# An attention pipeline whose routing follows one body sooner, with GpSimd's list of work and the ends of four stages rearranged

## The chip, the cores and the metric

The kernel runs on one NeuronCore of a Trainium2 chip. Its engines work at the same time, each on its own list of instructions: TensorE (PE; PEld is its loading of weights), VectorE (DVE), ScalarE (ACT), GpSimd (POOL) and SyncE (SP). They wait for each other through semaphores. The metric is the time of one execution on the device, in microseconds (us); the median of several executions counts.

## The reference

Four layers follow each other, each of them added to a running `x` of 32 batches x 256 rows x 128 columns: attention with an MLP, a mixture of experts, a recurrence, and the mixture of experts again with the same weights.

```python
x = x + attention(layernorm(x))     # 16 heads of 8, causal mask with a bias by distance; then relu MLP 128-512-128
x = x + experts(layernorm(x))       # 8 experts 128-256-128 (silu(gate) * up), the top 2 of the softmax, shares renormalised
x = x + recurrence(layernorm(x))    # gated scan over the rows, with its own layernorm
x = x + experts(layernorm(x))
```

For a mixture of experts `layernorm(x)` of each row is multiplied with the router's weights (128 x 8), the two largest of the 8 logits choose the experts, and the row's result is the sum of those two experts' outputs, weighted by their shares.

## The kernel before, in words

The program runs in stages that follow each other: a setup, attention, the experts ("first_"), the recurrence, the experts ("second_"), and a closing sum (`combine`). Each stage is a block in which every engine has a list of work written out by hand. A stage ends when all engines have reached its end: each engine drains its queue, all meet, and the semaphores are cleared. `phase` (L52 to L73) does the last part: it lets all engines meet in a barrier (L71), clears the semaphores (L72) and lets them meet again (L73).

**Attention** is a pipeline over 32 batches. Each engine's list is a function `body(b, n)`, called for `b` from -3 up to 32 plus `FULL` less one. In one body TensorE works at several batches at once: the scores of batch `b`, the maxima of `b + 1` and `b + 2`, the projection of `b + 3`, the MLP of `b - 2`, and the routing of batches further behind. A helper does nothing where its batch doesn't exist. Results of TensorE go to PSUM banks; two of them, T and W, are shared by many small matrix products. The tables `T_USES` and `W_USES` (L640 and L641) tell each user's place in the bank's turns and how many batches it lags, since the semaphores count by that.

Routing in attention works as follows, with the lag in bodies behind `b`:

- `finish(b - 2)` (L1094, VectorE) writes the finished `x` of a batch into `xres`.
- `row_stats` and `row_moments(b - 3)` (L1111, L1118, L1120, VectorE) give mean and variance; `row_root` and `row_apply(b - 3)` (L1511, L1523, GpSimd) turn them into normalised rows `d_rows`.
- `row_T` and `router(b - 4)` (L908, L917, TensorE) transpose the rows and multiply them with the router's weights; `take_rowT` and `take_logits(b - 4)` (L1329, L1338, ScalarE) take the results from PSUM.
- `sort`, `number`, `pick`, `members(b - 5)` (L175 to L193, VectorE) find the two largest logits; `rank(b - 5)` (L211, L214, TensorE) counts the rows that go to each expert; `place_a` to `place_d(b - 5)` (L220 to L248, VectorE) turn that into each row's place in a table in device memory. From `sort` on, the work is done once for two batches.
- `scatter` (L1543, GpSimd) sends the rows to those places by indirect DMAs, 128 rows each, the first choice (`b - 6`) and the second one (`b - 7`) in four DMAs each for every two batches. Before the second choice `relabel` (L244) overwrites the number that each row carries with it.

GpSimd has more in its body: `roots` and `norm_apply(b + 3)` (L1434, L1445) for the layernorm before attention, which wait for VectorE's `arg` of L997, and `second_root` and `second_apply(b - 1)` (L1472, L1482) for the layernorm before the MLP, followed by four short groups of additions.

**The experts** (`run_dispatched`) go over 72 tiles of 256 places: they load the rows of a tile with their expert's weights, multiply, and scatter the results back by indirect DMAs (L1669). ScalarE's function there is Silu (L1747); in the recurrence it uses a sigmoid (L2184) and an exponential. A function that isn't in the table loaded last needs an ACT_TABLE_LOAD first. The recurrence routes as well, and scatters at L2077. At the end of attention, of both runs of experts and of the recurrence, GpSimd waits until all its scatters have landed.

## Time and profile before

| | us |
|---|---|
| median of 3 runs | 1771.74 |
| lowest and highest | 1770.59, 1792.68 |
| profiled execution | 1777.81 |
| its span, first to last instruction | 1776.1 |
| mean granted clock of TensorE in it | 0.859 of full speed |

| stage | from, to (us of the span) |
|---|---|
| setup | 0, 87 |
| attention: first bodies without scatters | 87, 258 |
| attention: full bodies with scatters | 258, 833 |
| attention: the last batches leave the pipeline | 833, 908 |
| experts, first | 908, 1181 |
| recurrence | 1181, 1460 |
| experts, second | 1460, 1730 |
| closing sum | 1730, 1776 |

The profile was taken from one execution, so its parts add up to that execution's time and not to the median. A row of the timeline has the start, the duration, the engine, the line of the program, the operation, what it writes and reads, and in brackets how long the engine was idle before it and what released it. "x4" after a row means that four such instructions follow each other. An engine's name with a "q" is its queue: branches, drains and the issuing of DMAs. Neighbouring instructions of VectorE overlap by about 0.1 us.

### The profile page before, as it was taken

The numbers are of one execution on the slowest core, as the hardware profiler recorded it, in microseconds if no ns is written. First come the engines' busy times: TensorE is split into PE (matmuls) and PEld (weight loads), VectorE is DVE, ScalarE is ACT, GpSimd is POOL, SyncE is SP. The second block draws the span as 40 slices with busy tenths as digits, with TensorE's granted clock in tenths as the row PEclk, the third lists the DMA queues.
The fourth block names the chain that finished last, engine by engine and source line by source line (L and its number), as shares of the span: only waits on it lengthen the run. The fifth ranks groups of instructions, "written<-read, shape, count | busy, mean of one in ns | idle before, by whom it ended". The sixth has DMA issues, their size and how long they took to land. (4 is left out here: it accounts for less than half of the span.)

```text
span 1776.1 us, 37650 instructions
## 1 busy us (share of the span) xinstructions
PE 1367.7 (77%) x11633; PEld 1112.0 (63%) x11633; DVE 1253.9 (71%) x3903; ACT 782.6 (44%) x1751; POOL 960.0 (54%) x1156
## 2 busy tenths in 40 slices
PE   3699999999999999997447878847767618787850
PEld 2467777777677777765347878835555408787850
DVE  4379998989888888885455555548888835565637
ACT  1135555545445544544134444426666615444420
POOL 2214556656666566654645555533777754555540
PEclk9569999989899999998568998968787758988985
DMA  7101111111111111111232222211222122222218
GB/s 212 44 34 41 46 46 49 46 49 52 43 49 49 43 52 52 52 34 43 89 86 76 76 72 74 76 51 53 73 74 73 51 67 77 78 74 75 80 51 284
DMA packets 101873, 121.99 MB, mean 69 GB/s; under 512 B 18168, under 2 KB 81712, under 8 KB 101424
## 3 DMA queue, kind: packets, MB, share of 16 engines
q1 hardware_dynamic: 72592, 77.73, 14.7%
q0 software_dynamic: 17408, 36.21, 6.0%
q10 hardware_dynamic: 11680, 5.66, 1.2%
q8 instruction: 98, 1.61, 0.4%
q14 instruction: 95, 0.78, 0.1%
HBM read 49.72 MB, written 44.72 MB: 53 GB/s over the span
## 5 line engine op out<-in xcount | busy, mean ns | idle before, releaser
L1020 DVE TENSOR_REDUCE mx<-max_banks 128x6 f32<-128x768 f32 x256 | 243.1, 950 | 59.9 <-PE max_banks L769 46.0
L1049 DVE TENSOR_TENSOR ebuf<-score_banks,region 128x768 f32<-128x768 f32 x256 | 243.3, 950 | 27.3 <-PE score_banks L795 24.0
L1277 ACT ACTIVATE region<-ebuf 128x768 f32<-128x768 f32 x256 | 216.3, 846 | 101.4 <-DVE ebuf L1049 98.9
L1669 POOL DMA_INDIRECT choice_rows<-first_yo,first_xg x144 | 139.2, 967 | 132.5 <-DVE first_yo L1789 98.0
L1669 POOL DMA_INDIRECT choice_rows<-second_yo,second_xg x144 | 138.8, 964 | 130.5 <-DVE second_yo L1789 93.8
L2077 POOL DMA_INDIRECT expert_rows<-d_rows,z_d_index x128 | 130.7, 1021 | 38.8 <-issue 31.7
L1543 POOL DMA_INDIRECT expert_rows<-d_rows,a_d_index x128 | 129.1, 1009 | 36.9 <-issue 32.1
L757 PE MATMUL max_banks<-identb,region 128*128 128x128 bf16 x512 | 106.6, 231 | 29.5 <-DVE mx L1020 21.8
L1434 POOL TENSOR_TENSOR rs<-arg,neghalf 128x4 f32<-128x4 f32 x32 | 33.1, 1035 | 174.1 <-DVE arg L997 174.1
L814 PE MATMUL bankO<-region,vaug 128*32 128x256 f32 (+1 forms) x2048 | 124.5, 350 | 2.8 <-ACT region L1277 1.8
L1747 ACT ACTIVATE first_silu<-first_bgu,first_biases 128x256 f32<-128x256 f32 x144 | 63.6, 477 | 130.8 <-issue 48.4
L1781 DVE SCALAR_TENSOR_TENSOR first_hT<-first_bgu,first_biases,first_silu 128x256 f32<-128x256 f32 x144 | 65.0, 478 | 79.4 <-ACT first_silu L1747 58.0
L1747 ACT ACTIVATE second_silu<-second_bgu,second_biases 128x256 f32<-128x256 f32 x144 | 64.1, 477 | 128.7 <-issue 60.3
L1709 PE MATMUL second_by<-region,second_hT 128*128 x576 | 86.9, 300 | 41.8 <-DVE second_hT L1781 41.3
L1709 PE MATMUL first_by<-region,first_hT 128*128 x576 | 87.8, 301 | 37.6 <-DVE first_hT L1781 36.1
L1781 DVE SCALAR_TENSOR_TENSOR second_hT<-second_bgu,second_biases,second_silu 128x256 f32<-128x256 f32 x144 | 65.1, 478 | 72.0 <-ACT second_silu L1747 38.8
L791 PE MATMUL score_banks<-region_r 32*128 32x256 f32 x512 | 99.5, 386 | 18.2 <-DVE ebuf L1049 18.0
L1709 PEld LDWEIGHTS second_by<-region,second_hT 128*128 128x128 f32 x576 | 78.4, 211 | 47.5 <-issue 47.5
L1709 PEld LDWEIGHTS first_by<-region,first_hT 128*128 128x128 f32 x576 | 78.8, 212 | 45.2 <-issue 45.1
L761 PE MATMUL max_banks<-identb,region 128*128 128x128 bf16 x512 | 105.5, 229 | 0.0
L759 PE MATMUL max_banks<-identb,region 128*128 128x128 bf16 x512 | 105.5, 229 | 0.0
L765 PE MATMUL max_banks<-region_r 32*128 32x256 f32 x512 | 103.5, 401 | 0.0
(326 smaller groups left out, 4318.6 us busy)
## 6 DMA issues: line engine op xcount, KB each, us to landing
region_r<-region_r SPq DMA_DIRECT2D x192, 128.0 KB
first_xg<-expert_rows SPq DMA_DIRECT2D x72, 132.0 KB
second_xg<-expert_rows SPq DMA_DIRECT2D x72, 132.0 KB
z_rows<-choice_rows SPq DMA_DIRECT2D x32, 256.0 KB
c_rows<-choice_rows SPq DMA_DIRECT2D x16, 512.0 KB
out<-xres ACTq DMA_DIRECT2D x16, 256.0 KB
choice_rows<-first_yo,first_xg POOLq DMA_INDIRECT x144
choice_rows<-second_yo,second_xg POOLq DMA_INDIRECT x144
```

What stands on the lines that cost most here:

```text
L757: nc.tensor.matmul(r[:, hh, 0:P], biasb[:, h, P:2 * P], identb[:], start=True, stop=False, skip_group_check=True)
L759: nc.tensor.matmul(r[:, hh, P:2 * P], biasb[:, h, 0:P], identb[:], start=False, stop=False, skip_group_check=True)
L814: last = nc.tensor.matmul(bankO[VW * i:VW * (i + 1), g // 2, out:lo + 2 * P], vaug[:, n, kt, h, :], p32[:, (h // 2) % 4, h % 2, cols], sta ...
L1020: nc.vector.reduce_max(mx[:, n, places:places + 5:4, :], max_banks[:, :, 0:BK].rearrange("p h (k c) -> p h k c", k=3), AXX).then_inc(maxed ...
L1049: nc.vector.tensor_tensor(ebuf[:, half_of_ebuf(c, j), :, :], score_banks[:, :, 0:BK], bias32[:, plain(j), :], ALU.add).then_inc(scores_fre ...
L1277: nc.scalar.activation(p32[:, j % 4, :, :], ebuf[:, half_of_ebuf(c, j), :, :], ACT.Exp).then_inc(exped, 1)
L1543: pool.indirect_dma_start(slots_dram, bass.IndirectOffsetOnAxis(ap=d.index[:, m % 2, k, t:t + 1], axis=0), d.rows[:, (2 * m + t // 2) % DE ...
L1669: pool.indirect_dma_start(choice_dram, bass.IndirectOffsetOnAxis(ap=xg[:, i % G, t, E:E + 1].bitcast(I32), axis=0), yo[:, i % 4, t, :], No ...
L1709: last = nc.tensor.matmul(by[i % 2][:, t * E:(t + 1) * E], hT[:, i % 4, f, t * P:(t + 1) * P], w["down"][:, bass.ds(e, 1), f, :].rearrange ...
L1747: nc.scalar.activation(act_[:, f, :], bgu[i % 2 * NF + f][:, 0:2 * P], ACT.Silu, bias=biases[:, i % 4, f:f + 1]).then_inc(silu_done, 1)
L1781: nc.vector.scalar_tensor_tensor(hT[:, i % 4, f, :], bgu[i % 2 * NF + f][:, 2 * P:4 * P], biases[:, i % 4, NF + f:NF + f + 1], act_[:, f, ...
L2077: pool.indirect_dma_start(slots_dram, bass.IndirectOffsetOnAxis(ap=d.index[:, m % 2, k, t:t + 1], axis=0), d.rows[:, (2 * m + t // 2) % DE ...
```

## The change

It has five parts:

1. The routing in attention lags one body less from `row_T` on: `row_T`, `router` and their takers follow `b - 3`, sorting, ranking and placing `b - 4`, the scatters `b - 5` and `b - 6`. The bodies are one fewer (`FULL` 7), and the bank tables follow.
2. `row_stats` and `row_moments` stand near the start of VectorE's body, soon behind the `finish` of the same batch.
3. GpSimd's body begins with `row_root`, `row_apply` and `relabel`; of each group of four scatters two follow at once, the other two after `norm_apply`.
4. At the end of four stages SyncE waits for the landing of the scatters, GpSimd no longer does; and the barrier at L71 is gone, with the one behind the clearing kept.
5. ScalarE begins the experts' stages with a Silu of one column and the recurrence with a Sigmoid of one column, whose results nothing uses.

```diff
--- before.py
+++ after.py
@@ -68,7 +68,7 @@
 
     with ExitStack() as ctx:
         yield ctx, sem
-    nc.all_engine_barrier()
+
     nc.clear_and_free_semaphores(made)
     nc.all_engine_barrier()
 
@@ -636,9 +636,9 @@
     tabled, padded, z_loaded = sem("tables_made"), sem("rows_padded"), sem("z_loaded")
 
 
-    FIRST, FULL = -3, 8
-    T_USES = {"xmT": 2, "up": 2, "ot": 1, "row": 4, "oT": 1, "max": -1, "project": -3}
-    W_USES = {"project": -2, "up": 2, "ot": 1, "router": 4, "norm": -3, "rank": 5, "att": 1, "down": 2}
+    FIRST, FULL = -3, 7
+    T_USES = {"xmT": 2, "up": 2, "ot": 1, "row": 3, "oT": 1, "max": -1, "project": -3}
+    W_USES = {"project": -2, "up": 2, "ot": 1, "router": 3, "norm": -3, "rank": 4, "att": 1, "down": 2}
 
     def exists(c):
         return 0 <= c < B
@@ -946,15 +946,15 @@
                 turn(b - 1)
                 scores(b, n, 5)
                 scores_for_max(b + 1, after, 7)
-                row_T(b - 4)
+                row_T(b - 3)
                 weigh(b, n, 1)
-                router(b - 4)
+                router(b - 3)
                 out_T(b - 1)
                 scores(b, n, 6)
                 scores_for_max(b + 2, before, 0)
                 norm_T(b + 3)
                 weigh(b, n, 2)
-                rank(b - 5)
+                rank(b - 4)
                 max_T(b + 1, after)
                 scores_for_max(b + 2, before, 1)
                 scores(b, n, 7)
@@ -1172,17 +1172,19 @@
             def body(b, n):
                 after, before = (n + 1) % RING, (n - 1) % RING
                 reduce_max(b + 1, after, 3)
+                row_stats(b - 3)
                 add_mask(b, 1)
-                sort(b - 5)
+                row_moments(b - 3)
+                sort(b - 4)
                 reduce_max(b + 1, after, 4)
-                number(b - 5)
+                number(b - 4)
                 add_mask(b, 2)
-                pick(b - 5)
+                pick(b - 4)
                 take_low_xm(b - 2)
                 norm_stats(b + 3)
                 take_k(b + 2)
                 add_mask(b, 3)
-                members(b - 5)
+                members(b - 4)
                 reduce_max(b + 1, after, 5)
                 norm_moments(b + 3, n)
                 add_mask(b, 4)
@@ -1190,21 +1192,19 @@
                 normalise(b - 1)
                 add_mask(b, 5)
                 reduce_max(b + 1, after, 7)
-                row_stats(b - 3)
                 merge_max(b + 1, after)
-                row_moments(b - 3)
                 reduce_max(b + 2, before, 0)
                 add_mask(b, 6)
-                place_a(b - 5)
+                place_a(b - 4)
                 take_max(b + 1)
                 reduce_max(b + 2, before, 1)
-                place_b(b - 5)
+                place_b(b - 4)
                 second_norm(b - 1, before)
                 add_mask(b, 7)
-                place_c(b - 5)
+                place_c(b - 4)
                 second_moments(b - 1)
                 reduce_max(b + 2, before, 2)
-                place_d(b - 5)
+                place_d(b - 4)
                 take_q(b + 3)
                 finish(b - 2)
                 add_mask(b + 1, 0)
@@ -1357,9 +1357,9 @@
                 take_up_0(b - 2)
                 take_up_1(b - 2)
                 exponentials(b, 3)
-                take_rowT(b - 4)
+                take_rowT(b - 3)
                 exponentials(b, 4)
-                take_logits(b - 4)
+                take_logits(b - 3)
 
             for b in BODIES:
                 body(b)
@@ -1416,6 +1416,9 @@
                     sp.dma_start(z[name][:, t, :], bass.AP(tensor=v.tensor, offset=v.offset, ap=[[0, P], [1, s.E]])).then_inc(z_loaded, 16)
             sp.wait_ge(tabled, 1)
             pad_rows(sp, s, w, slots_dram, pads_dram, range(s.NE), padded)
+            for k in range(2):
+                for g in range(2):
+                    sp.wait_ge(scattered[k][g], 16 * B)
             sp.wait_ge(padded, 16 * s.NE)
             sp.wait_ge(z_loaded, 128)
 
@@ -1546,14 +1549,17 @@
 
             def body(b, n):
                 after, before = (n + 1) % RING, (n - 1) % RING
+                row_root(b - 3)
+                row_apply(b - 3)
+                relabel(b - 6)
+                for t in range(2):
+                    scatter(b - 5, 0, t)
+                    scatter(b - 6, 1, t)
                 roots(b + 3, n)
                 norm_apply(b + 3, n)
-                row_root(b - 3)
-                row_apply(b - 3)
-                relabel(b - 7)
-                for t in range(4):
-                    scatter(b - 6, 0, t)
-                    scatter(b - 7, 1, t)
+                for t in range(2, 4):
+                    scatter(b - 5, 0, t)
+                    scatter(b - 6, 1, t)
                 second_root(b - 1)
                 second_apply(b - 1)
                 biased_input(b - 1)
@@ -1563,9 +1569,6 @@
 
             for b in BODIES:
                 body(b, b % RING)
-            for k in range(2):
-                for g in range(2):
-                    pool.wait_ge(scattered[k][g], 16 * B)
 
 
 class ExpertWeights:
@@ -1670,8 +1673,6 @@
                             choice_dram, bass.IndirectOffsetOnAxis(ap=xg[:, i % G, t, E:E + 1].bitcast(I32), axis=0),
                             yo[:, i % 4, t, :], None,
                         ).then_inc(stored[i % 4], 16)
-                for q in range(4):
-                    pool.wait_ge(stored[q], 32 * ST // 4)
 
             @block.tensor
             def _(pe):
@@ -1747,6 +1748,8 @@
                         nc.scalar.activation(act_[:, f, :], bgu[i % 2 * NF + f][:, 0:2 * P], ACT.Silu,
                                              bias=biases[:, i % 4, f:f + 1]).then_inc(silu_done, 1)
 
+
+                nc.scalar.activation(act_[:, 0, 0:1], ident[:, 0:1], ACT.Silu)
                 for i in range(ST):
                     if i % 4 == 0:
                         e = experts_around(act, i)
@@ -1813,6 +1816,8 @@
                     sp.dma_start(xg[:, i % G, :, :].rearrange("p t c -> p (t c)"),
                                  slots_dram[bass.ds(first, s.Q), :].rearrange("(p t) c -> p (t c)", p=P)
                                  ).then_inc(arrived[i % G], 16)
+                for q in range(4):
+                    sp.wait_ge(stored[q], 32 * ST // 4)
 
 
 def combine(nc, s, xres, share, choice_dram, out):
@@ -2088,9 +2093,6 @@
                         scatter((i - 8) // 2, 1)
                     if placed_in(i) is not None:
                         scatter(placed_in(i), 0)
-                for k in range(2):
-                    for g in range(2):
-                        pool.wait_ge(scattered[k][g], 16 * B)
 
             @block.tensor
             def _(pe):
@@ -2222,6 +2224,8 @@
                         act.wait_ge(d_logits_full, b)
                     nc.scalar.copy(dT[:], bd[:, 0:2 * P]).then_inc(d_x_taken, 1)
 
+
+                nc.scalar.activation(z[:, 0, 0:1], ident[:, 0:1], ACT.Sigmoid)
                 for i in range(LAST):
                     q = i % 2
                     if sends(i - 1):
@@ -2256,6 +2260,9 @@
                 sp.wait_ge(tabled, 1)
                 pad_rows(sp, s, w, slots_dram, pads_dram, range(NE // 2, NE), padded)
                 sp.wait_ge(padded, 16 * NE)
+                for k in range(2):
+                    for g in range(2):
+                        sp.wait_ge(scattered[k][g], 16 * B)
 
 
 # ---- launch: one core; inputs and outputs as the reference has them ----
```

How GpSimd's list looks in a full body, with the name of what is written first. This is before, a body with four scatters:

```order
L1434 TENSOR_TENSOR rs<-arg,neghalf 128x4
L1445 TENSOR_SCALAR xn<-xres,mv,rs 128x128 x2
L1511 TENSOR_TENSOR rs<-arg,neghalf 128x2
L1523 TENSOR_SCALAR d_rows<-xres,mv,rs 128x128 x2
L244 CAST d_rows<-dest 128x4
L1543 DMA expert_rows<-d_rows,a_d_index 69632x132 x4
L1472 TENSOR_TENSOR rs<-arg,neghalf 128x2
L1482 TENSOR_SCALAR xm<-y,mv,rs 128x128 x2
L1492 TENSOR_TENSOR xb<-xres,b 128x128 x2
L1465 TENSOR_TENSOR xlb<-xlb,outb 128x128 x2
```

And this is the change, over the same work:

```order
L1514 TENSOR_TENSOR rs<-arg,neghalf 128x2
L1526 TENSOR_SCALAR d_rows<-xres,mv,rs 128x128 x2
L244 CAST d_rows<-dest 128x4
L1546 DMA expert_rows<-d_rows,a_d_index 69632x132 x2
L1437 TENSOR_TENSOR rs<-arg,neghalf 128x4
L1448 TENSOR_SCALAR xn<-xres,mv,rs 128x128 x2
L1546 DMA expert_rows<-d_rows,a_d_index 69632x132 x2
L1475 TENSOR_TENSOR rs<-arg,neghalf 128x2
L1485 TENSOR_SCALAR xm<-y,mv,rs 128x128 x2
L1495 TENSOR_TENSOR xb<-xres,b 128x128 x2
L1468 TENSOR_TENSOR xlb<-xlb,outb 128x128 x2
```

The rows' root and normalisation (L1511, now L1514) and the relabelling stand ahead of the four-column root (L1434, now L1437), and the scatters are in two runs of two.

VectorE around `finish` (L1094), which is followed by the next body, before:

```order
L1094 TENSOR_TENSOR xres<-bankTW,ysum 128x256
L1049 TENSOR_TENSOR ebuf<-score_banks,region 128x768
L1020 TENSOR_REDUCE mx<-max_banks 128x2x3
L1049 TENSOR_TENSOR ebuf<-score_banks,region 128x768
L175 MAX sorted<-a_d_logits 128x8 x4
L1020 TENSOR_REDUCE mx<-max_banks 128x2x3
L180 MAX_INDEX a_d_order<-sorted,a_d_logits 128x8 x4
L1049 TENSOR_TENSOR ebuf<-score_banks,region 128x768
L186 TENSOR_TENSOR a_d_hot<-a_d_order,iota 128x4x2x8
L1101 TENSOR_TENSOR xmlo<-bankTW,xmhi 128x256
```

Before, the statistics of finished rows (L1111, L1118, L1120) stood in the middle of the body:

```order
L1049 TENSOR_TENSOR ebuf<-score_banks,region 128x768
L1020 TENSOR_REDUCE mx<-max_banks 128x2x3
L1111 BN_STATS stats<-xres 128x6 x2
L1030 TENSOR_TENSOR mq<-mx 128x16
L1118 BN_AGGR mv<-stats 128x2 x2
L1120 TENSOR_SCALAR arg<-mv 128x2
L1020 TENSOR_REDUCE mx<-max_banks 128x2x3
```

With the change:

```order
L1094 TENSOR_TENSOR xres<-bankTW,ysum 128x256
L1049 TENSOR_TENSOR ebuf<-score_banks,region 128x768
L1020 TENSOR_REDUCE mx<-max_banks 128x2x3
L1111 BN_STATS stats<-xres 128x6 x2
L1049 TENSOR_TENSOR ebuf<-score_banks,region 128x768
L1118 BN_AGGR mv<-stats 128x2 x2
L1120 TENSOR_SCALAR arg<-mv 128x2
L175 MAX sorted<-a_d_logits 128x8 x4
L1020 TENSOR_REDUCE mx<-max_banks 128x2x3
L180 MAX_INDEX a_d_order<-sorted,a_d_logits 128x8 x4
L1049 TENSOR_TENSOR ebuf<-score_banks,region 128x768
L186 TENSOR_TENSOR a_d_hot<-a_d_order,iota 128x4x2x8
```

The statistics have moved behind `finish`, ahead of the sort (L175) and `xmlo` (L1101).

## Rows read from the trace of the kernel before

**Rows 1.** Busy time and instructions of each engine by stretch, granted clock, DMA share, GB/s

```profile
258.00:833.00 575.00, 536.33 (x5664) 404.40 (x5665) 487.77 (x1220) 282.70 (x544) 358.09 (x483) 0.96 0.14 46
833.00:908.00 75.00, 26.55 (x147) 21.48 (x146) 31.36 (x138) 8.49 (x22) 47.51 (x57) 0.59 0.31 97
```

**Rows 2.** Starts of VectorE's `xmlo` (L1101) before the scatters, and beside them

```profile
L1101 DVE TENSOR_TENSOR xmlo<-bankTW,xmhi x3: 415/416/420, 202.4 to 246.3; 128x256 fp32r<-128x256 f32 x3
L1101 DVE TENSOR_TENSOR xmlo<-bankTW,xmhi x23: 414/416/420, 269.7 to 795.8; 128x256 fp32r<-128x256 f32 x23
```

**Rows 3.** Waits, 150 to 833 us: engine, line, releaser, total us, times, longest us

```profile
DVE mx L1020 <- PE max_banks L769: 22.1, 29, 0.9
DVE xres L1094 <- remote: 18.2, 22, 1.7
DVE mx L1020 <- remote: 12.1, 11, 2.4
```

**Rows 4.** Timeline of VectorE, `finish`: start us, us, operation, [idle before <-releaser]

```profile
241.44 0.41 DVE L1094 TENSOR_TENSOR xres<-bankTW,ysum 128x256 f32<-128x256 f32 x1
...
530.60 0.42 DVE L1094 TENSOR_TENSOR xres<-bankTW,ysum 128x256 f32<-128x256 f32 x1 [1.19 <-remote]
```

**Rows 5.** Timeline of VectorE, middle of a body

```profile
520.50 0.48 DVE L1111 BATCH_NORM_STATS2 stats<-xres 128x6 f32<-128x128 f32 x2
...
521.01 0.25 DVE L1118 BATCH_NORM_AGGREGATE mv<-stats 128x2 f32<-128x6 f32 x2
...
522.25 0.96 DVE L1020 TENSOR_REDUCE mx<-max_banks 128x6 f32<-128x768 f32 x1 [0.79 <-PE max_banks L769]
```

**Rows 6.** Timeline of GpSimd in the same body

```profile
521.55 0.72 POOL L1511 TENSOR_TENSOR rs<-arg,neghalf 128x2 f32<-128x2 f32 x1 [2.73 <-DVE arg L1120]
...
524.37 1.11 POOL L1543 DMA_INDIRECT expert_rows<-d_rows,a_d_index  x1 [0.29 <-POOL d_rows L244]
...
529.29 0.75 POOL L1472 TENSOR_TENSOR rs<-arg,neghalf 128x2 f32<-128x2 f32 x1
```

**Rows 7.** Timeline of VectorE and GpSimd, drain of attention

```profile
850.50 0.21 DVE L1087 TENSOR_SCALAR arg<-mv 128x2 f32<-128x2 f32 x1
...
853.31 0.74 POOL L1472 TENSOR_TENSOR rs<-arg,neghalf 128x2 f32<-128x2 f32 x1
...
867.19 0.42 DVE L1094 TENSOR_TENSOR xres<-bankTW,ysum 128x256 f32<-128x256 f32 x1 [8.98 <-PE bankTW L897]
...
868.98 0.48 DVE L1111 BATCH_NORM_STATS2 stats<-xres 128x6 f32<-128x128 f32 x2
...
872.85 1.11 POOL L1543 DMA_INDIRECT expert_rows<-d_rows,a_d_index  x1 [0.29 <-POOL d_rows L244]
...
902.89 0.96 POOL L1543 DMA_INDIRECT expert_rows<-d_rows,a_d_index  x1 [0.30 <-issue]
```

**Rows 8.** Ends of stages by line: xcount, ns min/median/max, first and last start us

```profile
L697 POOLq COMPARE_BRANCH  x1: 37/37/37, 905.3 to 905.3; - x1
L697 POOLq DRAIN  x1: 2022/2022/2022, 905.5 to 905.5; - x1
...
L1662 POOLq DRAIN  x2: 2989/2990/2992, 1177.1 to 1726.6; - x2
...
L71 POOLq DRAIN  x4: 34/34/46, 1180.3 to 1775.3; - x4
L71 SPq EVENT_SEMAPHORE  x4: 17/17/17, 1180.6 to 1775.6; - x4
```

**Rows 9.** Timeline of ScalarE and VectorE around the table loads

```profile
914.07 1.28 ACT L1747 ACT_TABLE_LOAD   x1 [1.32 <-PE first_bgu L1700]
...
1193.81 1.28 ACT L2184 ACT_TABLE_LOAD   x1
...
1196.71 0.43 DVE L2006 SCALAR_TENSOR_TENSOR z_relu<-z_sig,z_relu 128x256 f32<-128x256 f32 x1 [1.18 <-ACT z_relu L2187]
```

**Rows 10.** Waits, 908 to 1180 us, columns as in rows 3

```profile
ACT first_silu L1747 <- remote: 44.9, 13, 6.4
```

## The prediction

> **What bounds the kernel now.** I read the table of stages first [rows 1]. From 258 to 833 us, the full bodies of attention, TensorE is busy 536 of 575 us and VectorE 488: the two take turns as the limit. GpSimd, busy 358, has room. From 833 to 908 TensorE works 27 of 75 us and GpSimd 48: attention drains through GpSimd. So an edit is worth something in three places: in a body, where it touches the engine that limits that part of it; in the drain of attention; and at the ends of the stages.
>
> Next, the body. Its `xmlo` instruction runs once a body [rows 2]. Before any scatter the three starts from 202.4 to 246.3 are 43.9 / 2 = 21.95 us apart; with scatters, 23 starts from 269.7 to 795.8 give 526.1 / 22 = 23.91 us. The waits [rows 3] say what came with the scatters. VectorE waits 18.2 us at `finish` (`xres` L1094) and 12.1 us at a `mx` reduction for "remote", a releaser that the profile can't name. That is 30.3 us over 575 / 23.9 = 24 bodies, 1.26 us each. Two rows point to the scatters: `finish` at 241.44, before the first of them, starts without idle time; at 530.60 it has waited 1.19 us [rows 4], and a group of four scatters ran from 524.37 to 529.29, just ahead [rows 6]. I read this as TensorE's signal coming late while scatters are in flight beside `mlp_down`.
>
> Who limits which part: before `mx` at 522.25 VectorE idles 0.79 us for TensorE [rows 5], and it does so 29 times, 22.1 us [rows 3]; there TensorE is the bound. From `finish` at 530.60 to the next `xmlo` nearly no wait of VectorE is listed; there VectorE is the bound.
>
> **The change, part by part.**
>
> 1. *Row statistics move.* `row_stats` (L1111, 0.48 us) and `row_moments` (L1118, 0.25 us, and L1120, shorter still) [rows 5] take some 0.9 us of VectorE, 0.7 after the usual overlap of neighbours by 0.1. They leave the stretch where VectorE idles for TensorE and go behind `finish`, where it doesn't idle. There they show in full: +0.7 us a body. What they give back at the old place only lengthens the 0.79 us of idleness. Over 24 bodies that is +16.8, and in 4 earlier bodies +2.8.
>
> 2. *GpSimd's order.* With the statistics ready about 2.5 us behind `finish` instead of in the middle of the next body, root and rows (0.8 + 1.6 us, as from 521.55 [rows 6]) come some 10 us earlier, and the first two scatters of each group of four run before `roots`, the other two behind `norm_apply`. Today four in a row hold `second_root` until 529.29 [rows 6]; afterwards two shorter runs end before it. Beside `mlp_down` no scatter is left, so the late signal at `finish` should go: -1.26 a body. But now two scatters run beside other TensorE work, at two new places. What that costs, S us a body, no row shows. Its ends: 0 (nothing waits there within a signal's delay), and 1.9, both mean waits for "remote" in one body (18.2 / 22 + 12.1 / 11 [rows 3]). Nothing below zero: the scatters are as many as before. A run half as long should stall half as long, if at all, and part of the new places lies where VectorE has slack; I take half of 1.26, S = 0.6.
>
>    Items 1 and 2 per body: 0.70 - 1.26 + 0.6 = +0.04, over 24 bodies +1.0, and the +2.8.
>
> 3. *A body less lag.* Scatters, `sort` and `number` begin one body earlier, so one full body more carries them: S once, +0.6, and +0.7 for the sorting (the period grew by 1.96; 1.26 of it is the late signal, 0.7 the rest). `row_T` needs the rows in the middle of a body, where they are made today; they will be there 5 us ahead, so nothing new waits. Full bodies so far: 1.0 + 2.8 + 0.6 + 0.7 = +5.1.
>
> 4. *The drain of attention* [rows 7]. `second_root` of the last batch starts at 853.31, though its `arg` was there at 850.71: it stands behind four scatters. The change sends these earlier: -2.6, and `finish` at 867.19, the end of TensorE's chain from it, follows. The last `row_stats` starts at 868.98, since a sort stands between it and `finish`, which ended at 867.61; it will come first: -1.4. After the last rows five groups of four scatters are sent, from 872.85 to 903.85; one lag less leaves four, and a group takes 529.29 - 524.37 = 4.9: -5.0 with its wait. Sum -9.0. The bounds are 2 us to either side: SyncE's padding rows hang on the same chain and may land later than the scatters, or the scatters may wait less for each other's landing than today.
>
> 5. *Ends of stages* [rows 8]. GpSimd's last scatter of attention ends at 903.85, its branch comes at 905.3 and its drain of 2.02 us at 905.5; the stage ends with it. With the wait for the landing on SyncE, GpSimd drains 1.35 us sooner. The recurrence and both runs of experts end in the same way: 4 x -1.35 = -5.4. Bounds: 0, if the drain itself waits for the landing (then it only grows), and -5.4. I take -5.4, since at L1662 the drain lasts 2989 and 2992 ns in two stages with different data: it looks like a fixed duration and not like the rest of a transfer.
>
>    The barrier at L71 lasts from 1180.3 to 1180.6, and its twin at L73 stays: 4 x -0.3 = -1.2.
>
> 6. *Table loads* [rows 9]. The one at 1193.81 takes 1.28 us, and VectorE idles 1.18 us for what follows it, at 1196.71; at the start of the stage ScalarE waits for data anyway: -1.2. The Silu load at 914.07 comes after 1.32 us of waiting for TensorE, which is the later engine there: 0 for it and its twin, at best -1.3 each.
>
>    Sum: -9.0 - 5.4 - 1.2 - 1.2 = -16.8 outside the full bodies, and +5.1 in them: **-11.7 us**.
>
> The profiled execution took 1777.8 us, 6 us above the median; against it the sum gives 1766.1, against the median of 1771.7 it gives **1760**.
>
> **Rivals.** They differ in S and in what the late signal is.
>
> *A, the stall vanishes* (S = 0): two scatters at a time between GpSimd's arithmetic hold up nobody. -16.8 - 24 x 0.56 + 2.8 + 0.7 = -27 us, 1745. For it: VectorE's waits for "remote" stand at two places only. Against: scatters go with late signals in the first run of experts too, where ScalarE waited 44.9 us for "remote" in 13 places [rows 10]. Chance 0.17.
>
> *B, the stall moves and grows* (S = 1.9), the slower side. At the start of a body VectorE is the bound, and in its middle TensorE; if each pair of scatters delays a signal of TensorE there, VectorE waits twice a body, on top of the 0.7 us of row work: -16.8 + 24 x (1.9 - 0.56) + 2.8 + 1.9 + 0.7 = +21, **1792**. It turns slower than before from S = 1.1 (25 S = 16.8 + 13.4 - 3.5 = 26.7). For it: the 1.19 us at 530.60 show that nothing absorbs a late signal. Against: the shorter runs. Chance 0.15.
>
> *C, the scatters never were the cause*: the late signal at `finish` belongs to TensorE's own order in bodies that also route, and stays. Then only the row work is felt: -16.8 + 24 x 0.7 + 3.5 = +3 us, 1775. For it: routing starts within a body or two of the scatters. Against: the delay shows just behind each run of scatters. Chance 0.13. The Trainium skill ("SBUF — State Buffer", Who interferes with whom) is on its side: a DMA never contends with a compute engine, and TensorE never waits on anyone.
>
> *D, the drains wait for the landing*: 5.4 us less gain, else my forecast: 1766. Chance 0.1.
>
> **How the numbers follow.** The forecast has 0.45. Its own range: S from 0.2 to 1.0 moves it 10 us either way, the drain of attention 2, the loads 2 down: 1748 to 1773. To leave no more than 2 in 10 out I go down to 1740 (A, and 5 below it) and up to 1786 (C and D whole, part of B). Two per cent is about what a measurement of this kernel can tell from no change. Faster by more means under 1736.3: A with all its savings larger, 0.06. Slower by more is over 1807.2: B with S near 2.5, 0.03. The same: 0.91. B and C lie above 1771.7, the rest, 0.72, below it.
>
> **What the profile after would show.** Item 1: VectorE's `stats` L1111 right behind `finish` without idle time, and 0.7 us more from `finish` to `xmlo`. Item 2: no wait for "remote" at `xres` L1094; if B holds, such waits stand at other lines, over 40 us in all; if C holds, 18 us stay at L1094. The period of `xmlo` decides: near 23.9 my forecast, 23.4 A, 25.2 B, 24.6 C. Item 4: four groups of scatters behind the last rows, and the stage's end 10.4 us nearer to the last full body. Item 5: GpSimd's drain begins 0.2 us behind its last scatter and lasts 2.02 us; in D it lasts 3.4. Item 6: no wait of VectorE for `z_relu` over 0.2 us. The forecast is wrong if TensorE's granted clock, 0.96 in the full stretch [rows 1], falls with the new spacing; no term here has that in it.

## The result, and the profile after

| | before | changed |
|---|---|---|
| median of 4 runs | 1779.70 us | 1801.44 us |
| lowest, highest | 1770.59, 1792.68 | 1798.31, 1805.23 |
| span of the profiled execution | 1776.1 us | 1797.8 us |

The ratio is 1.0125, with a 95% interval of 1.0082 to 1.0168: slower, by 22 us, where I had forecast 12 us less. (The median of before is of four runs here; the three known ahead of the prediction had 1771.74.) The two traces, cut at the starts of `xmlo` and at GpSimd's drains, say where (in us, each stretch after less before):

| stretch | before | after | difference |
|---|---|---|---|
| start to first `xmlo` | 139.6 | 139.9 | +0.3 |
| `xmlo` of batch 0 to 5, few scatters or none | 106.7 | 118.2 | +11.5 |
| batch 5 to 27, full bodies | 526.4 | 539.9 | +13.5 |
| batch 27 to 29 | 45.8 | 57.3 | +11.5 |
| batch 29 to 31 | 38.4 | 38.4 | 0 |
| `xmlo` of batch 31 to the last scatter | 47.0 | 40.4 | -6.6 |
| last scatter to the end of the drain | 3.7 | 2.3 | -1.3 |
| the four stages behind attention | 868.6 | 861.4 | -7.2 |

So the ends came out about as forecast, the drain of attention gained somewhat less, and the bodies lost, the first ones too. First the starts of `xmlo` in the full bodies, then VectorE's longest waits from 150 to 833 us, after, the rows that answer to [rows 2] and [rows 3]:

```profile
L1101 DVE TENSOR_TENSOR xmlo<-bankTW,xmhi x22: 409/412/417, 281.7 to 798.0; 128x256 fp32r<-128x256 f32 x22
```

```profile
DVE mx L1020 <- PE max_banks L769: 50.2, 32, 4.1
...
DVE ebuf L1049 <- remote: 23.6, 12, 2.0
```

The mean period is 516.3 / 21 = 24.59 us. Undisturbed bodies take 23.3 and 24.7 us in turn (the second with the sorting), where before they took 23.05 and 23.51: 24.0 for 23.28, +0.7 a body. No wait of `xres` for "remote" is left, as forecast; the wait stands at another line, `ebuf` L1049, as rival B said. The timelines show its making, first GpSimd's, then TensorE's (the scores that `ebuf` waits for), then VectorE's of the same body:

```profile
577.90 1.09 POOL L1546 DMA_INDIRECT expert_rows<-d_rows,a_d_index  x1 [0.17 <-issue]
579.30 0.96 POOL L1546 DMA_INDIRECT expert_rows<-d_rows,a_d_index  x1 [0.30 <-issue]
```

```profile
578.90 0.22 PE L795 MATMUL score_banks<-region_r 32*128 32x128 f32 x2
```

```profile
580.98 0.96 DVE L1049 TENSOR_TENSOR ebuf<-score_banks,region 128x768 f32<-128x768 f32 x1 [1.98 <-remote]
...
586.95 0.96 DVE L1020 TENSOR_REDUCE mx<-max_banks 128x6 f32<-128x768 f32 x1 [1.35 <-PE max_banks L769]
```

TensorE's last matmul for these scores starts at 578.90 and is over some 0.2 us later, as the profile models its end. The run of two scatters ends at 580.26, and only 0.7 us later does VectorE get the signal it had waited for since 579.0. Nearly all of this wait is lateness of the signal. At `finish` there is nothing to see now, and the row work stands behind it as intended:

```profile
618.19 0.41 DVE L1094 TENSOR_TENSOR xres<-bankTW,ysum 128x256 f32<-128x256 f32 x1
...
620.25 0.47 DVE L1111 BATCH_NORM_STATS2 stats<-xres 128x6 f32<-128x128 f32 x2
```

The last full bodies ran with TensorE's clock partly at its lower level, 0.73 on the mean; the second row is that of before, its last full bodies. Between the starts of `xmlo` of batch 27 and 29 alone the means are 0.73 after and 0.95 before. In the middle, 300 to 780 us, the clock is no reason for the loss: 0.98 after, 0.96 before.

```profile
780.00:862.00 82.00, 71.55 (x601) 53.20 (x597) 49.78 (x126) 31.88 (x60) 36.95 (x52) 0.73 0.07 23
```

```profile
780.00:833.00 53.00, 42.94 (x431) 31.70 (x420) 35.34 (x91) 24.05 (x44) 28.11 (x38) 0.88 0.04 14
```

The end of the attention stage: GpSimd's last scatter, and its drain.

```profile
933.10 0.96 POOL L1546 DMA_INDIRECT expert_rows<-d_rows,a_d_index  x1 [0.30 <-issue]
```

```profile
L697 POOLq DRAIN  x1: 7339/7339/7339, 929.1 to 929.1; - x1
```

A drain of 7.3 us, where [rows 8] had 2.0, looks like a loss and isn't: it is entered at 929.1, while scatters are still being worked off, and ends at 936.4, 2.3 us behind the last one (934.06). Before, the same distance was 907.5 - 903.85 = 3.7 us. And at the start of the recurrence no table load stands between ScalarE's copy and its first gate any more, so `z_relu` follows without idle time, the answer to [rows 9]:

```profile
1220.42 0.37 ACT L2180 COPY z_xT<-zx 128x256 f32<-128x256 f32 x1 [0.78 <-PE zx L2102]
1220.68 0.48 ACT L2186 ACTIVATE z_gate<-zk,z_cols 128x256 f32<-128x256 f32 x1
```

```profile
1222.44 0.42 DVE L2011 SCALAR_TENSOR_TENSOR z_relu<-z_sig,z_relu 128x256 f32<-128x256 f32 x1
```

### The profile page after: what moved, and what is told of

It is laid out like the page before. It is cut to its first block and busy times, and to the rows that moved or that the text cites. A ratio compares the mean times of both kernels' runs of the same rounds, so it can differ in the third digit from the quotient of the medians.

```text
span 1797.8 us, 37606 instructions
## 1 busy us (share of the span) xinstructions
PE 1381.4 (77%) x11633; PEld 1118.3 (62%) x11633; DVE 1250.7 (70%) x3903; ACT 781.6 (43%) x1754; POOL 963.5 (54%) x1156
## 5 line engine op out<-in xcount | busy, mean ns | idle before, releaser
L1049 DVE TENSOR_TENSOR ebuf<-score_banks,region 128x768 f32<-128x768 f32 x256 | 242.8, 948 | 54.8 <-PE score_banks L795 29.7
L1475 POOL TENSOR_TENSOR rs<-arg,neghalf 128x2 f32<-128x2 f32 x32 | 23.2, 723 | 269.4 <-DVE arg L1087 269.4
L757 PE MATMUL max_banks<-identb,region 128*128 128x128 bf16 x512 | 108.6, 234 | 30.7 <-DVE mx L1020 23.8
L814 PE MATMUL bankO<-region,vaug 128*32 128x256 f32 (+1 forms) x2048 | 121.3, 358 | 4.7 <-ACT region L1277 3.4
L759 PE MATMUL max_banks<-identb,region 128*128 128x128 bf16 x512 | 107.5, 232 | 0.0
L761 PE MATMUL max_banks<-identb,region 128*128 128x128 bf16 x512 | 107.5, 232 | 0.0
```

The costliest lines, as they stand in the source:

```text
L757: nc.tensor.matmul(r[:, hh, 0:P], biasb[:, h, P:2 * P], identb[:], start=True, stop=False, skip_group_check=True)
L759: nc.tensor.matmul(r[:, hh, P:2 * P], biasb[:, h, 0:P], identb[:], start=False, stop=False, skip_group_check=True)
L814: last = nc.tensor.matmul(bankO[VW * i:VW * (i + 1), g // 2, out:lo + 2 * P], vaug[:, n, kt, h, :], p32[:, (h // 2) % 4, h % 2, cols], sta ...
L1049: nc.vector.tensor_tensor(ebuf[:, half_of_ebuf(c, j), :, :], score_banks[:, :, 0:BK], bias32[:, plain(j), :], ALU.add).then_inc(scores_fre ...
```

## The experiments

Each ratio is to the kernel before on the same chip. It turned out that chips come in two kinds, and every result has to be read by kind. The medians of the kernel before were 1779.7, 1790.95 and 1772.91 us on chips of one kind (I call them chips L, for late signals of TensorE), and 1625.21, 1619.78 and 1620.27 us on those of the other (chips P, prompt). Bodies are given as "without / with sorting", the usual ones.

| kernel | scatters stand | chips L: ratio, bodies | chips P: ratio, bodies |
|---|---|---|---|
| before | 4, ahead of `second_root`, late | 1, 23.05 / 23.51 | 0.9998, 22.26 / 23.04 |
| changed | 2 + 2 | 1.0125 and 1.0001, 23.3 / 24.7 | 0.9834 and 0.9895, 22.28 / 22.92 |
| changed places, old lags and ends | 2 + 2 | 1.0067, 23.2 / 24.6 | 0.9869, 22.29 / 22.91 |
| VectorE's row work moved alone | 4, 3 us earlier | 1.0318, 25.4 to 28.9 | 0.9858, 22.29 / 22.82 |
| changed, unparted | 4, behind `norm_apply` | 1.0345, 26.6 / 27.7 | 0.988, 22.28 / 22.92 |
| changed, at the body's end | 4 | not run | 1.0015 and 1.0017, 22.3 / 23.9 |
| changed, singles | 1 + 1 + 1 + 1 | 0.9798, 22.46 / 23.04 | not run |
| ends alone | as before | not run | 0.9886, as before |
| ends, new places in the drain only | as before | 0.9935 and 0.9896, 23.0 / 23.5 | not run |

**The ends alone.** Edit: parts 4 and 5 of the change, nothing in attention's bodies.

```diff
-    nc.all_engine_barrier()
     nc.clear_and_free_semaphores(made)
...
-                for k in range(2):
-                    for g in range(2):
-                        pool.wait_ge(scattered[k][g], 16 * B)
...
+                        sp.wait_ge(scattered[k][g], 16 * B)
```

> The kernel before with parts 4 and 5 of the change alone: the waits at the ends of four stages on SyncE, one barrier less in each, the tables loaded at the starts of stages. Attention's bodies are those of before. Theory 1 (the loss lies in attention's bodies): drains 4 x -1.35, barriers 4 x -0.3, Sigmoid -1.2: about -8 us against before. Theory 2 (GpSimd's drain instruction of 7.3 us, where it was 2.0, is time lost): 4 x +4 = +16 us, with stages that end 5 to 6 us behind their last scatter, where before they ended 3.7 to 4.6 behind it.

Measured on a chip P: 0.9886 (0.9837 to 0.9934). The stages end 2.3 and 3.0 us behind their last scatters, where the kernel before ended 3.6 and 4.5 behind them; the four stages behind attention are 6.5 us shorter in all than in the control's profile below. Theory 1 holds in its sign and theory 2 falls. But the interval means 11 to 26 us less, more than the 8 us that the profile accounts for; where the rest comes from stays open. A profile alone can't tell it: the stretch ahead of the first `xmlo`, in which this kernel and the one before differ in nothing, takes 139.5, 139.6 and 144.6 us in the three profiles of them.

**VectorE's row work alone.** Edit, against before:

```diff
                 reduce_max(b + 1, after, 3)
+                row_stats(b - 3)
                 add_mask(b, 1)
+                row_moments(b - 3)
...
                 reduce_max(b + 1, after, 7)
-                row_stats(b - 3)
                 merge_max(b + 1, after)
-                row_moments(b - 3)
```

> The kernel before with VectorE's row_stats and row_moments alone moved behind finish; GpSimd's list, the lags and the ends as before. Theory 1a (the stretch from finish to xmlo is bound by VectorE and the row work shows in full): that stretch grows from 4.87 to about 5.4 us, the period of the body by 0.5 to 0.7, some +17 us in all over 28 bodies; the wait for remote at finish stays near 18 us. Theory 1b (the row work is free, the loss is all of scatters at new places): period unchanged, 0 us.

> The kernel before with VectorE's row work alone moved behind finish. Without late signals it came out at 0.986, though I had expected it slower; its bodies took 22.3 and 22.8 us, 0.1 less than those of the control, and its last bodies 78.0 us for the control's 83.9. If that is real it repeats here: 0.985 to 0.99 on a 1620 us chip. On a 1780 us chip the 0.53 us from finish to xmlo come on top of the late signal at finish: bodies near 23.8, +10 us.

On a chip P the period isn't longer: 22.29 / 22.82 for 22.26 / 23.04 us. The stretch from `finish` to `xmlo` takes 5.39 us, but there the control's took 5.37 already, with a wait of 0.5 to 0.6 us for TensorE in it; the row work took that wait's place. My +0.7 a body was wrong for the full bodies. In the five bodies from batch 0 to 5, where there is little else to wait for, it shows: 109.5 us for the control's 106.7, +2.8. And the edit alone is 0.9858 (0.9795 to 0.9921) there, as good as the whole change on chips P, so what the parts gain on them doesn't add up: its profile is 6.5 us shorter than the control's from batch 5 to 27 and 5.9 from 27 to 31, for a reason that no run isolates. On a chip L the same edit is 1.0318 (1.0239 to 1.0396), the bodies 25.4 to 28.9 us, 26.5 on the mean. The longest waits of VectorE for "remote" there, 300 to 780 us:

```profile
DVE mx L1020 <- remote: 27.8, 17, 3.9
```

**The places with the old lags.** Edit: the one above, and GpSimd's order of the change with `b - 6` and `b - 7` kept; the ends as before.

> The kernel before with VectorE's row work moved and GpSimd's new order (rows first, scatters in two runs of two), but every lag as before, one body more in the drain, and the ends as before. Theory 1 (row work 0.53 to 0.75 us, and a stall of about 1.3 us at new places for 1.26 us at the old one): period of the body near 24.0 us as in the changed kernel, for 23.3 before: +0.7 x 26, +17 us, less 4 in the drain of attention: +13. Theory 3 (the shorter lag itself costs, by what the bank tables make TensorE wait for): period near 23.3, about -4 us.

> The kernel before with the changed kernel's places on VectorE and GpSimd, but every lag and the ends of before. Where signals are late: bodies as the changed kernel's, 23.3 and 24.7 us, and 1.005 to 1.02, if the places cost and not the lag; bodies near 23.3 if the lag has the cost. Where they aren't: 0.987 again.

0.9869 (0.9808 to 0.993) on a chip P, 1.0067 (1.0035 to 1.01) on a chip L, with the changed kernel's bodies there, within 0.1 us. So the places make the slower bodies, and the shorter lag has no part in them.

**The changed kernel again, and a control** (the kernel before, unaltered, measured like a changed one).

> The changed kernel once more, unaltered, on the chip of the other runs. +1.2% against before, as known. What is open is TensorE's granted clock: it was 0.67 from 800 to 820 us and 0.59 from 840 to 860, in the last two full bodies, which took 29.4 and 27.9 us where the ones ahead took 24. If that belongs to the change, it comes back in this profile, some 10 us; if it is chance, the last full bodies take 24 to 25 us and the half-clock stretch lies elsewhere.

> The kernel before, unaltered, measured like a changed one. In the runs so far the time of this program depended on the chip: 1780 us on one, 1625 on another, where four different kernels all came out 1.1 to 1.7% below it. If that is what an edit gives, this control has a ratio of 1.000; if the comparison itself leans by a per cent to the kernel under test, this one shows it too (0.985 to 0.99). Its profile says whether VectorE's waits for remote at finish (18 us) and the half-clock bodies are there on this chip.

> The changed kernel, unaltered, beside the control. If scatters delay TensorE's signals on this chip (waits for remote in the control), the period of its bodies is 0.7 us above the control's and the ratio about 1.01; if they don't, both periods are near 22.6 us, and the ratio is 1 less what drains, barriers and the shorter drain of attention give: about -8 -9 = -17 us, 0.99.

> The changed kernel, unaltered, in the hope of a chip on which the kernel before takes near 1780 us, as where the change was first timed. There, theory 1 expects 1.01 again, with bodies of 23.3 and 24.7 us and waits of VectorE for remote; on a chip where the kernel before takes near 1620 us, 0.99, with bodies of 22.3 and 22.9 us and none of these waits, as in both runs so far.

The control reads 0.9998 (0.9968 to 1.0027), so the comparison doesn't lean. The changed kernel wins on chips P, 0.9834 (0.9764 to 0.9905) and 0.9895 (0.9844 to 0.9945). On chips L it was 1.0125 and, on another one, 1.0001 (0.9962 to 1.004); the usual bodies are the same in both profiles, and why only one of these chips shows a loss stays open. In no profile of a chip P does VectorE wait for "remote" in the full bodies.

The name "remote" stands only where a signal comes more than 1.5 us behind TensorE's matmul, so I give the lateness itself too, as the traces have it: the time of the signal less the modelled end of its matmul. On a chip P, in the control and in the changed kernel, none of the 256 signals of the maxima (L769) and the 256 of the scores (L795) is more than 0.05 us late. In the first profile of the changed kernel, on a chip L, all 28 signals of the scores given beside a run of scatters are late, by 0.9 to 1.9 us; of the 41 of the maxima beside a run 18 are late and 23 aren't. So a run delays many of TensorE's signals, and not all. In the kernel before 21 signals of the maxima are late, most by 0.9 us, and yet arrive while the run is on.

For the slow pair of bodies at the end, the answer is mixed: on the second chip L the two bodies behind batch 27 took 26.8 and 27.5 us (its profile is of the longest of ten executions, 1813.11 us where the median is 1794.04), on chips P 21.7 and 21.0 to 25.0. A clock below 0.9 there isn't bound to chips L: from batch 27 to 29 it was 0.73 and 0.78 in the changed kernel on them, and 0.85 and 0.96 on chips P. Two other kernels with moved row work have one such body each (32.0 and 30.0 us), on chips L, the unparted kernel there has none, nor have those with the full bodies of before.

**Scatters in one run.** Edit, against the changed kernel:

```diff
-                relabel(b - 6)
-                for t in range(2):
-                    scatter(b - 5, 0, t)
-                    scatter(b - 6, 1, t)
                 roots(b + 3, n)
                 norm_apply(b + 3, n)
-                for t in range(2, 4):
+                relabel(b - 6)
+                for t in range(4):
```

> The changed kernel, but its four scatters stand in one run behind norm_apply, ahead of second_root, where they stood before; rows, lags and ends as changed. Theory 1 (with signals delayed, each run of scatters costs about a microsecond whatever its length, and two runs cost two): where the control shows waits for remote, the period falls from the changed kernel's 24.0 to 23.3-23.5, -12 us against it. Theory 4 (a stall is as long as the scatters are many): period as changed, 24.0. Where the control has no such waits both say: no difference.

> The changed kernel with its four scatters in one run behind norm_apply. It was 0.988 of the kernel before where signals weren't late, and the changed kernel 0.9895, so no difference there. On a 1780 us chip theory 1 (a run of scatters costs about 1 to 1.3 us whatever its length) expects bodies near 23.4 us, -12 us against the changed kernel; theory 4 (the stall is as long as the scatters are many) expects 24.0, no difference.

On a chip P no difference, 0.988. On a chip L 1.0345 (1.0275 to 1.0415): theory 1, a fixed price for a run, falls. The timelines of GpSimd, TensorE and VectorE there show how the price is made:

```profile
589.18 0.96 POOL L1546 DMA_INDIRECT expert_rows<-d_rows,a_d_index  x1 [0.30 <-issue]
590.44 0.96 POOL L1546 DMA_INDIRECT expert_rows<-d_rows,a_d_index  x1 [0.30 <-issue]
```

```profile
589.24 0.22 PE L769 MATMUL max_banks<-region_r 32*128 32x128 f32 x2
```

```profile
587.93 0.20 DVE L1030 TENSOR_TENSOR mq<-mx 128x16 f32<-128x16 f32 x1
592.25 0.96 DVE L1020 TENSOR_REDUCE mx<-max_banks 128x6 f32<-128x768 f32 x1 [4.12 <-remote]
```

VectorE stands from 588.13 to 592.25, until 0.85 us behind the last of the four scatters. TensorE's matmuls for these maxima are over at about 589.5, so 2.8 us of the 4.1 are lateness and the rest is TensorE's own work. This is the 0.7 us of the changed kernel's pair again: the signal arrives when the run is through. Theory 5, in what follows, takes this for all of TensorE's signals beside a run, which is too much: in the same profile 25 of those of the weighing (L814), late too, arrive while the run is on. The same four scatters of the kernel before began some 5 us later in the body, beside `mlp_down`, and what VectorE waited at `finish` behind them was 1.2 us. What set that time had been `row_moments` in mid-body, for which GpSimd waited [rows 6]. With it moved, alone or in the unparted kernel, the same four scatters begin 3 or 5 us earlier and the time is 1.03; with the scatters parted as well it is 1.0001 on the same chip. That the place is the reason is argued from these traces; the runs that were to test it fell on chips P, as the gated runs below show.

A part of the loss may be the clock's: from 300 to 780 us the granted clock is 0.88 in this kernel and 0.92 in the one with the row work alone, on the same chip, where the kernel before with the new drain and ends has 0.97 (all of one chip L). The runs don't part it from the wait.

**Scatters at the end of GpSimd's body.** Edit, against the changed kernel: `relabel` and four scatters behind `residuals`, in one run.

> The changed kernel, but relabel and all four scatters at the end of GpSimd's body, behind the residuals, so that they run beside the first third of the next body and not beside mlp_down. If the place decides what a late signal costs, this is the worst or the best of the orders: at the start of the body VectorE is the bound and has no slack, so with late signals I expect a period of 24.0 to 24.5; by the theory that only the number of runs counts, 23.3 to 23.5. Without late signals no difference to the changed kernel but its drain, +5 us.

> The changed kernel with relabel and four scatters at the end of GpSimd's body. On a 1620 us chip it was 1.0015, bodies with scatters up to 25.4 us. On a 1780 us chip theory 5 expects a run of four beside the scores of the next body, where VectorE and ScalarE wait for a signal of TensorE every microsecond: 3 to 4 us late in each body, 26 us and more, 1.03 or worse. If instead only the stretch beside the router is bad, bodies stay near 24 us.

Both runs fell on chips P: 1.0015 and 1.0017. Where signals are prompt a run can still be in the way. It ran into the next body and held `row_root` up; TensorE waits for the rows, 300 to 780 us:

```profile
PE bankTW L908 <- POOL d_rows L1526: 10.2, 10, 1.0
```

What it does on a chip L was not seen.

**Timing given back by a wait (the gated runs).** Edit, against the unparted kernel (and, as the second run, against the one with the row work alone moved), ahead of `relabel`:

```diff
+                if exists(b + 1):
+                    pool.wait_ge(T_free, useT("max", b + 1) + 1)
                 relabel(b - 6)
```

> The changed kernel, but its four scatters stand in one run behind norm_apply as in the unparted one, and GpSimd waits ahead of them for VectorE's take_max (L1036), after which the scatters of the kernel before began. Theory 5 (a run of scatters holds TensorE's signals until it is through, so its place in the body is all; the moved row_moments had been the clock that put it beside mlp_down): on a 1780 us chip bodies of 23.1 and 23.5 us as before, where unparted had 26.6 and 27.7, and 0.985 to 0.99 of the kernel before, 60 us less than unparted. Theory 6 (what costs is the row work in VectorE's bound stretch and the rows' earlier root): bodies over 26 us as unparted. On a 1620 us chip 0.985 to 0.99 by both.

> The kernel before with VectorE's row work moved behind finish, as stats_only, and the same wait of GpSimd for take_max ahead of relabel and scatters; lags and ends as before. Theory 5, on a 1780 us chip: the ratio falls from 1.032 to 0.995-1.003, bodies of 23.1 to 23.6 us; what is left above the control's bodies is the price of the row work itself (0.53 us from finish to xmlo, if it shows at all). Theory 6: it stays at 1.03. On a 1620 us chip 0.985 to 1.00.

Both ran on a chip P, so theory 5 wasn't put to the test, and both failed my other expectation: 1.0341 (1.0306 to 1.0376) and 1.0358 (1.0317 to 1.0399), bodies of 23.6 and 27.5 us. `take_max` comes late: the scatters then hold `second_root`, and TensorE waits up to 1.5 us a body for `xm`. First that wait, then the clock in the full bodies of this kernel and of the control:

```profile
PE bankTW L861 <- POOL xm L1485: 28.4, 19, 1.5
```

```profile
300.00:780.00 480.00, 449.76 (x4447) 350.08 (x4446) 391.68 (x977) 218.36 (x426) 284.46 (x386) 0.86 0.13 45
```

```profile
300.00:780.00 480.00, 453.12 (x5022) 348.86 (x5022) 435.52 (x1084) 246.50 (x478) 317.11 (x427) 0.99 0.15 50
```

The control waits there too, 15.2 us in 21 bodies. With 0.8 us more of this wait a body the granted clock of the stretch is 0.86 instead of 0.99, and the bodies are 3.1 us longer on the mean (25.96 for 22.84).

**One scatter at a time.** Edit, against the changed kernel, with the pairs resolved:

```diff
                 row_apply(b - 3)
                 relabel(b - 6)
+                scatter(b - 5, 0, 0)
+                scatter(b - 6, 1, 0)
                 roots(b + 3, n)
                 norm_apply(b + 3, n)
+                scatter(b - 5, 0, 1)
+                scatter(b - 6, 1, 1)
                 second_root(b - 1)
                 second_apply(b - 1)
+                scatter(b - 5, 0, 2)
+                scatter(b - 6, 1, 2)
...
                 residuals(b - 1)
+                scatter(b - 5, 0, 3)
+                scatter(b - 6, 1, 3)
```

> The changed kernel with its four scatters apart, one each behind row_apply, norm_apply, second_apply and the residuals. Theory 5 as it stands (a run holds TensorE's signals until it is through): where signals are late, one scatter holds them about 1 us, so four places cost at most four times that, less where an engine had slack; with 0.5 us each, bodies of 23.5 to 24.5 us, 0.99 to 1.01, no worse than the changed kernel. If every run costs its 1.2 to 2 us however short, bodies of 26 us, 1.03. Where signals are not late: as the changed kernel, 0.99, if second_apply's two parts stay ahead of TensorE's need.

On a chip L: 0.9798 (0.974 to 0.9856), 1738.47 us for 1772.91, the fastest kernel on chips L. The changed kernel wasn't run on this chip; the one with its places and the old lags and ends had 1.0067 there. Its bodies, 22.46 / 23.04 us, are within 0.1 to 0.2 us of those of chips P. Its starts of `xmlo`, and VectorE's longest waits from 300 to 780 us:

```profile
L1101 DVE TENSOR_TENSOR xmlo<-bankTW,xmhi x22: 407/410/413, 271.8 to 750.5; 128x256 fp32r<-128x256 f32 x22
```

```profile
DVE mx L1020 <- PE max_banks L769: 28.9, 21, 1.4
```

22.80 us on the mean, and no row for "remote" at all. The wait of 1.4 us that is left is there on chips P too (28.6 us in 21 bodies, changed kernel), so it is TensorE's own work. Single scatters still delay signals, but little: of the maxima's 256 signals 2 are over 0.15 us late, the later by 0.55, and of those of the weighing (L814), 128, 14 are, by at most 0.71. Four of them cost 0.1 to 0.2 us a body in all; I had allowed 0.5 us each.

**Old full bodies, new drain and ends.** Edit: the ends, and the changed kernel's places of row work and scatters only `if b >= B`.

> The kernel before with the ends of the change, and with VectorE's and GpSimd's new places only in the bodies from 32 on, where no scores are left to compute; the full bodies and all lags are those of before. If what the change gives lies in ends and drain alone: -8 for the ends, as ends_only (-12 in its profile), and -4 more in the drain of attention (second_root and the last statistics no longer behind other work): 0.985 to 0.99 on a 1620 us chip, 0.99 on a 1780 us one. If the full bodies give the gain of stats_only, it stays 5 us or more above that kernel's time less 8.

> The kernel before in its full bodies, with the changed ends and the new places only from body 32 on. Where signals are late it was 0.9935. Where they aren't, ends_only had 0.989 and the changed kernel 0.984 to 0.9895: I expect 0.985 to 0.99 here, so that it would be no slower than the changed kernel on either kind of chip.

Both ran on chips L: 0.9935 (0.9896 to 0.9973) and 0.9896 (0.9847 to 0.9945). So the drain and the ends are worth 12 to 18 us even there; the changed kernel lost them again in its bodies. Chips P haven't seen this one.

## Why the prediction was wrong

**The step that failed** is item 2's S, "a run half as long should stall half as long, if at all, and part of the new places lies where VectorE has slack; I take half of 1.26, S = 0.6". Against the bodies of chips P, which have no late signals, the changed bodies pay 23.3 - 22.28 = 1.0 and 24.7 - 22.92 = 1.8 us, S = 1.4; against the bodies with single scatters on a chip L it is 0.8 and 1.7, S = 1.25. The idea that length counts was right (one scatter costs next to nothing, two 1.0 and 1.8, four in that region about 4.5, of which the lower clock has an unknown part), but I took the wait behind one run at one place for the price of a run anywhere. Rival B named the mechanism, and I gave it 0.15. Its +21 us is the measured +22 almost exactly, and that is luck: it had S = 1.9 and the row work in full, and nothing for the clock.

**The same row misled on the gain.** I counted 1.26 us a body of "remote" waits as recoverable. Against chips P the kernel before pays 23.28 - 22.65 = 0.63 us; the other half would be waiting for TensorE without them. A wait that goes is worth less than its length where another one stands behind it.

**Row work, +0.7 a body**: wrong in the other direction. It shows between `finish` and `xmlo` (5.39 us for 4.87 on chips L), and the period of the full bodies on chips P doesn't grow. For the bodies ahead of the scatters the forecast of +2.8 was right (+2.8 from batch 0 to 5). With both corrections the balance per full body is -0.63 + 0 + 1.4 = +0.8, for the +0.04 forecast and the +0.7 read off the traces. That is no test of its own, as both terms come from the same bodies.

**What I left out**: that `row_moments` was GpSimd's clock for the scatters. Item 1 priced its move on VectorE alone. By the edit with that alone on a chip L, it was the dearest part of the change, +3.2%, and the parting that I had weighed as a risk repaired it. I left out the first bodies too, but for the row work: from batch 0 to 5 the changed kernel takes 7.2 us more than the control on a chip P as well (113.9 for 106.7).

**The clock**: the prediction named it as what would make it wrong. Over the full stretch, 258 to 833 us, it didn't fall: 0.96 as before. The last full bodies, at 0.73, add 11.5 us in the profile, one body of 28.8 us among the first ones, at 0.82, 4 more; nearly half of the 33 us between forecast and result lies there. How much of this is the change's own doing the runs don't settle, as the two ratios on chips L, 1.0125 and 1.0001, differ by more than their intervals.

**The drain of attention, -9.0**: it came out smaller. From batch 29 to the last scatter it is -6.7 us in the first pair of profiles, and -5.8 and -5.7 in the two of the changed kernel on chips P against the control's; from batch 27 on it is -8.5 in one (130.9 to 122.4 us) and -4.4 in the other. My bounds were -7 to -11. **Ends of stages, -5.4**: the distances shrank by 1.3, 1.5, 1.3 and 1.5 us, sum 5.6. Right in size; the sign that I gave for it (a drain of 2.02 us) was wrong, and rival D would have been accepted on the drain's length alone. **Barriers and Sigmoid, -2.4**: the stages behind attention gave 7.2 us, of which 4.3 are drains; the rest, 2.9, is about right. **Rival C fell**: singles and the runs in the wrong places show that scatters are the cause. The rule of the Trainium skill that it leaned on ("SBUF — State Buffer", Who interferes with whom) speaks of ports and data; TensorE did work on beside the scatters (L769 at 589.24, L795 at 578.90, as far as modelled ends tell), and what came late was its signal, so the rule isn't refuted here, but it didn't give the time.

## What to carry to other kernels

Before an instruction is moved, ask who waits for it as a clock: an engine whose other work is timed by that wait moves too, and its DMAs land beside other work. A late signal costs by what is waited for while it is held, not by how long a run lasts elsewhere; if DMAs that GpSimd issues must be spread, spread them singly, which one run of four executions on one chip L bears out here. And measure on more than one chip: this change gains 1.05 and 1.66% on two chips of one kind and loses 1.25% and nothing on two of the other.

## What the runs showed of the hardware

On some chips many of the signals that TensorE gives beside a run of GpSimd's indirect DMAs come late: those of the scores by 0.9 to 1.9 us with two DMAs, those of the maxima by 2.4 to 2.8 us with four. Those that outlast the run come 0.5 to 0.8 us behind its end with two, 0.9 us with four behind `norm_apply`, 1.4 us with four at `finish`. With single DMAs the most is 0.7 us, among the maxima and the weighing. On the other chips the same programs have no signal of scores or maxima more than 0.05 us late. The kernel before takes 1773 to 1791 us on the first kind and 1620 to 1625 on the second. Most of that lies in the experts' stages, which also scatter: 272.6 and 270.2 us in the profile with late signals, 200.2 and 202.3 in the control's. What makes a chip of the one or the other kind stays open; no run here varied it. GpSimd's drain may begin while its DMAs are still being worked off, so that its duration says nothing about what it costs; the distance from the last DMA to the end of the stage does.
